# Recommender tower: two of the seven input blocks of dense layer 1 summed inside the interaction loop

## The reference

```python
e = jnp.stack([tbl_0[ids[:, 0]], ..., tbl_39[ids[:, 39]]], axis=1)
vi = e[:, i_idx, :]
vj = e[:, j_idx, :]
viW = jnp.einsum('bpd,pde->bpe', vi, W)          # W: 780 x 64 x 64
z = jnp.einsum('bpe,bpe->bp', viW, vj)           # 512 x 780
h = jnp.concatenate([z, dense_ctx], axis=1)      # 512 x 796
h = jnp.maximum(h @ W_top1 + b_top1, 0.0)        # 512 x 512
h = jnp.maximum(h @ W_top2 + b_top2, 0.0)        # 512 x 256
y = h @ W_top3                                   # 512 x 1
```

## Time and profile before

| | |
|---|---|
| median of 3 executions | 322.66 us (322.57, 322.66, 323.78) |
| span of the profiled execution | 320.2 us, 4340 instructions |
| its own time outside the span | not given apart; the median lies 2.5 us above the span |
| PE busy | 312.7 us (98%) |
| DVE busy | 252.3 us (79%) |
| POOL busy | 237.7 us (74%) |
| ACT busy | 90.3 us (28%) |
| granted TensorE clock | full in every slice (2.4 GHz) |

### The profile page before, as it was taken

How to read it: one execution, slowest core, us unless ns; L and a number is a source line. 1 busy time by engine, 2 the same in 40 slices (tenths; PEclk the granted TensorE clock), 3 DMA queues, 4 the chain that set the end, 5 groups by cost and what they waited for, 6 DMA issues and landing times.

```text
span 320.2 us, 4340 instructions
## 1 busy us (share of the span) xinstructions
PE 312.7 (98%) x1716; PEld 117.5 (37%) x1716; DVE 252.3 (79%) x243; ACT 90.3 (28%) x206; POOL 237.7 (74%) x178
## 2 busy tenths in 40 slices
PE   6899999999999999999999999999999999989996
PEld 2465233332333323333333333333333333323464
DVE  4995987788689888988898899999999999940000
ACT  0203500600106835559976363000000000000032
POOL 3898777777777777776677999999999999940000
PEclk9999999999999999999999999999999999999999
DMA  6981332323323753232323121221121000000000
GB/s 136 358 243 21 82 72 62 92 59 67 87 57 92 253 171 86 61 93 57 88 60 90 41 66 34 66 68 46 52 68 57 0 2 0 0 3 5 12 0 0
DMA packets 14459, 23.27 MB, mean 73 GB/s; under 512 B 3556, under 2 KB 4584, under 8 KB 14312
## 3 DMA queue, kind: packets, MB, share of 16 engines
q1 hardware_dynamic: 7848, 13.96, 15.6%
q0 software_dynamic: 4096, 4.20, 6.4%
q10 hardware_dynamic: 2496, 4.84, 4.5%
HBM read 22.86 MB, written 0.00 MB: 71 GB/s over the span
## 4 chain that ended last, share of the span: by engine, by line
PE 65%; POOL 28%; DMA 3%; DVE 1%; POOLq 1%; ACT 0%; issue 0%; ACTq 0%
PE y_ps L611 33%; POOL prod L352 28%; PE z_ps L632 16%; PE y_ps L642 5%; PE y_ps L535 3%; DMA prod<-in_tbl 2%; PE t_ps L642 2%; PE y_ps L682 2%; PE t_ps L535 2%; PE t_ps L587 1%; DMA prod<-hot_ids 1%; DVE prod L522 1%; POOLq L185 1%; PE t_ps L682 1%; DVE x_quad L463 0%; PE y_ps L691 0%
## 5 line engine op out<-in xcount | busy, mean ns | idle before, releaser
L611 PE MATMUL y_ps<-x,w 64*128 64x512 f32 x780 | 183.3, 605 | 0.2
L336 POOL DMA_INDIRECT gathered<-in_tbl,ids_sb x128 | 130.6, 1020 | 45.7 <-issue 28.5
L522 DVE TENSOR_TENSOR prod<-y_ps,x 128x1024 f32<-128x1024 f32 x89 | 103.2, 1218 | 20.5 <-PE y_ps L611 20.1
L522 DVE TENSOR_TENSOR prod<-y_ps,x_quad 128x1024 f32<-128x1024 f32 x96 | 110.7, 1217 | 4.4 <-PE y_ps L611 3.7
L611 PEld LDWEIGHTS y_ps<-x,w 64*128 64x128 f32 x780 | 70.0, 186 | 108.3 <-issue 79.1
L352 POOL TENSOR_TENSOR prod<-prod 128x1024 f32<-128x1024 f32 x46 | 106.9, 2374 | 0.3
L632 PE MATMUL z_ps<-prod,select 128*32 128x512 f32 x596 | 74.5, 600 | 1.3 <-POOL prod L352 1.3
L389 ACT COPY x<-x_fold 32x128 f32<-32x128 f32 x112 | 33.1, 296 | 18.1 <-DVE x_fold L491 16.9
L632 PEld LDWEIGHTS z_ps<-prod,select 128*32 128x32 f32 x596 | 14.4, 108 | 54.1 <-issue 37.6
L418 ACT COPY zT<-z_ps 128x512 f32<-128x512 f32 x6 | 3.5, 586 | 100.6 <-PE z_ps L632 100.6
L412 ACT COPY x_mix<-x 64x512 f32<-64x512 f32 x40 | 24.7, 617 | 0.7
(11 more groups left out here) (46 smaller groups left out, 87.5 us busy)
## 6 DMA issues: line engine op xcount, KB each, us to landing
w<-w_rows SPq DMA_DIRECT2D x48, 256.0 KB, 2.7
gathered<-in_tbl,ids_sb POOLq DMA_INDIRECT x128, 2.5
w<-w_rows ACTq DMA_DIRECT2D x1, 1792.0 KB, 8.0
prod<-in_tbl ACTq DMA_DIRECT2D x6, 256.0 KB, 8.5
prod<-hot_ids SPq DMA_DIRECT2D x4, 256.0 KB, 6.7
prod<-in_tbl ACTq DMA_DIRECT2D x4, 128.0 KB, 3.1
w<-w_rows ACTq DMA_DIRECT2D x1, 512.0 KB, 9.7
w<-w_rows SPq DMA_DIRECT2D x1, 192.0 KB, 2.3
```

What stands on the lines that cost most here:

```text
L336: nc.gpsimd.indirect_dma_start(gathered[:, slot, c, s * DIM:(s + 1) * DIM], None, tables[f][:, :], bass.IndirectOffsetOnAxis(ap=ids_sb[:, ...
L522: nc.vector.tensor_tensor(prod[:, d % PROD_SLOTS, :, :], y_ps[:, d % DUO_SLOTS, :, :], factor, ALU.mult).then_inc(prod_ready, 1)
L611: last = nc.tensor.matmul(y_ps[:, d % DUO_SLOTS, half, :], w[rows, r % W_SLOTS, d % ROUND, :], x[rows, units[half], :], start=True, stop=True)
```

## The change

Blocks 0 and 1 of layer 1 (all four column groups, 8 matmuls of 128x128 weights with 512 columns) move into rounds 18 to 25, one per round, ahead of the round's last duo, with `t_ps` as their bank. The order is m = 1, 2, 3, 0, two rounds each. After m = 1, 2 and 3 ACT copies the bank to the new tile `h1_part` (`save_part`, at the head of ACT's rounds 20, 22 and 24); the sums of m = 0 stay in `t_ps` and are continued at the end. So `t_ps` isn't free from round 18 on, and units 18 and 19, which PE transposed there in rounds 26 and 28, go the way of `FOLDED` (now 11 to 19).

Behind the loop `rest` is blocks 2 to 5. Their matmuls are put in between `sum_round(47)` and `sum_round(48)` in another order, block 6 of m = 1, 2, 3, 0 follows, and m = 3 and m = 0 end last. DVE adds `h1_part` to the banks of m = 1, 2 and 3 in place, and ACT's ReLU reads the result; that of m = 0 still reads `t_ps`. Layer 2 takes its inputs in the order 1, 2, 3, 0.

```diff
-FOLDED = range(11, 18)
+FOLDED = range(11, 20)
+EARLY_BLOCKS = 2
+EARLY = {18 + EARLY_BLOCKS * n + b: (m, b) for n, m in enumerate((1, 2, 3, 0)) for b in range(EARLY_BLOCKS)}
...
+            def save_part(m):
+                act.wait_ge(part_summed, m)
+                nc.scalar.copy(h1_part[:, m - 1, :], t_ps[:, :]).then_inc(part_saved, 1)
...
+                if r - 1 in EARLY:
+                    m, b = EARLY[r - 1]
+                    if m and b == EARLY_BLOCKS - 1:
+                        save_part(m)
...
-            for m in range(M1):
-                act.wait_ge(h1_summed, m + 1)
-                nc.scalar.activation(h1[m], h1_ps[m], ACT.Relu, bias=b1[:, m:m + 1]).then_inc(h1_ready, 1)
+            for m in range(1, M1):
+                act.wait_ge(h1_added, m)
+                nc.scalar.activation(h1[m], h1_part[:, m - 1, :], ACT.Relu, bias=b1[:, m:m + 1]).then_inc(h1_ready, 1)
+            act.wait_ge(h1_summed, M1)
+            nc.scalar.activation(h1[0], h1_ps[0], ACT.Relu, bias=b1[:, 0:1]).then_inc(h1_ready, 1)
...
+            dve.wait_ge(part_saved, M1 - 1)
+            for m in range(1, M1):
+                dve.wait_ge(h1_summed, m)
+                nc.vector.tensor_tensor(h1_part[:, m - 1, :], h1_part[:, m - 1, :], h1_ps[m], ALU.add).then_inc(h1_added, 1)
...
+            def layer1_early(m, b):
+                if m == 1 and b == 0:
+                    pe.wait_ge(w1_loaded, 32)
+                    pe.wait_ge(z_saved, EARLY_BLOCKS)
+                    pe.wait_ge(x_ready, FOLDED.start)
+                elif b == 0:
+                    pe.wait_ge(part_saved, m - 1 if m else M1 - 1)
+                done = nc.tensor.matmul(t_ps[:, :], w1[:, b, m * ROWS:(m + 1) * ROWS], zT[:, b, :],
+                                        start=b == 0, stop=m > 0 and b == EARLY_BLOCKS - 1)
+                if m and b == EARLY_BLOCKS - 1:
+                    done.then_inc(part_summed, 1)
...
+                    if r in EARLY and d == ROUND * r + ROUND - 1:
+                        layer1_early(*EARLY[r])
                     interact(d)
...
-            sum_round(len(plan.rounds) - LAG)
-            pe.wait_ge(w1_loaded, 32)
-            full = list(range(NBLK - 1))
-            layer1(0, full[:-1], first=True)
-            pe.wait_ge(z_saved, NBLK - 1)
-            layer1(0, full[-1:])
-            for r in range(len(plan.rounds) - LAG + 1, len(plan.rounds)):
-                sum_round(r)
-            for m in range(1, M1 - 1):
-                layer1(m, full, first=True)
-            for m in range(M1 - 1):
-                layer1(m, [NBLK - 1], last=True).then_inc(h1_summed, 1)
-            layer1(M1 - 1, [NBLK - 1], first=True)
-            layer1(M1 - 1, full, last=True).then_inc(h1_summed, 1)
+            rest = list(range(EARLY_BLOCKS, NBLK - 1))
+            pe.wait_ge(z_saved, NBLK - 2)
+            layer1(0, rest[:-1])
+            sum_round(len(plan.rounds) - LAG)
+            pe.wait_ge(prod_ready, ROUND * (len(plan.rounds) - 1) + 1)
+            layer1(1, rest[:1], first=True)
+            sum_round(len(plan.rounds) - 1)
+            layer1(1, rest[1:-1])
+            layer1(2, rest[:-1], first=True)
+            pe.wait_ge(z_saved, NBLK - 1)
+            layer1(1, rest[-1:])
+            layer1(2, rest[-1:])
+            pe.wait_ge(dense_loaded, 16 * M1)
+            pe.wait_ge(last_copied, 16 * 4 * M1)
+            layer1(1, [NBLK - 1], last=True).then_inc(h1_summed, 1)
+            layer1(2, [NBLK - 1], last=True).then_inc(h1_summed, 1)
+            layer1(3, [NBLK - 1], first=True)
+            layer1(0, [NBLK - 1])
+            layer1(3, rest, last=True).then_inc(h1_summed, 1)
+            layer1(0, rest[-1:], last=True).then_inc(h1_summed, 1)
```

More of the change, by code:

```diff
@@ L214, in dlrm_tower @@
         head = sb("head", [ROWS, M1 + M2 + M2 * QUAD])
+        h1_part = sb("h1_part", [ROWS, 3, BATCH])
         y_out = sb("y_out", [ROWS, BATCH // 4])
@@ L273, in dlrm_tower @@
         z_saved = sem("z_saved")
+        part_summed = sem("part_summed")
+        part_saved = sem("part_saved")
         last_copied = sem("last_copied")
         h1_summed = sem("h1_summed")
+        h1_added = sem("h1_added")
         h1_ready = sem("h1_ready")
@@ L659, in _ @@
                     sum_round(r - LAG)
+            rest = list(range(EARLY_BLOCKS, NBLK - 1))
+            pe.wait_ge(z_saved, NBLK - 2)
+            layer1(0, rest[:-1])
             sum_round(len(plan.rounds) - LAG)
-            pe.wait_ge(w1_loaded, 32)
-            full = list(range(NBLK - 1))
-            layer1(0, full[:-1], first=True)
-            pe.wait_ge(z_saved, NBLK - 1)
-            layer1(0, full[-1:])
-            for r in range(len(plan.rounds) - LAG + 1, len(plan.rounds)):
-                sum_round(r)
-            for m in range(1, M1 - 1):
-                layer1(m, full, first=True)
+            pe.wait_ge(prod_ready, ROUND * (len(plan.rounds) - 1) + 1)
[3 more added lines that the diff above has]
+            layer1(2, rest[:-1], first=True)
+            pe.wait_ge(z_saved, NBLK - 1)
+            layer1(1, rest[-1:])
+            layer1(2, rest[-1:])
             pe.wait_ge(dense_loaded, 16 * M1)
             pe.wait_ge(last_copied, 16 * 4 * M1)
-            for m in range(M1 - 1):
-                layer1(m, [NBLK - 1], last=True).then_inc(h1_summed, 1)
-            layer1(M1 - 1, [NBLK - 1], first=True)
-            layer1(M1 - 1, full, last=True).then_inc(h1_summed, 1)
+            layer1(1, [NBLK - 1], last=True).then_inc(h1_summed, 1)
[4 more added lines that the diff above has]
+            layer1(0, rest[-1:], last=True).then_inc(h1_summed, 1)
             def layer2(n, m):
-                for k in range(M1):
+                for turn, k in enumerate((1, 2, 3, 0)):
                     if n == 0 and m == 0:
-                        pe.wait_ge(h1_ready, k + 1)
+                        pe.wait_ge(h1_ready, turn + 1)
                     last = nc.tensor.matmul(h2_ps[n][m][:, batch_halves[n]], w2[:, k, m * ROWS:(m + 1) * ROWS],
-                                            h1[k][:, batch_halves[n]], start=(k == 0), stop=(k == M1 - 1))
+                                            h1[k][:, batch_halves[n]], start=(turn == 0), stop=(turn == M1 - 1))
                 last.then_inc(h2_summed, 1)
```

## The result

The changed kernel takes 326.98 us (median of four, 325.91 to 330.08) where the kernel before takes 322.62: a ratio of 1.0152, 95% interval 1.01 to 1.0203: slower by 1 to 2%. The prediction was 326.4. The profiled execution has a span of 325.4 us, predicted 323.9; the fastest one, with a mean granted clock of 1.0, has 324.0. The kernel before has slower executions at a lower mean clock too: of 23 in a later run the five at 0.989 took 325.75 to 327.98 us, the others 321.45 to 325.17.

A forecast was written before the change was run, and what follows sets the result against it. PE was taken to bound rounds 18 to 25, PE, DVE and POOL all full in rounds 28 to 47, PE alone behind the loop. Terms: 9.4 - 5.9 + 0.2 = +3.7 on 322.66, giving 326.4 us; 8-in-10 range 323.8 to 328.0.

The forecast's parts named there:

- One early matmul costs 1.27 us in the loop, 10.2 for eight: Rounds 18 to 25: each early matmul adds 0.86 us plus edges of 0.20 and 0.21; eight add 10.2 us.
- the two parts (0.20 and 0.21): Loop edges per early matmul: 0.20 us from tail blocks between sums, 0.21 us from product runs cut by transposes.
- The rival that the edges are free: Rounds 18 to 25: eight early matmuls cost only 6.9 us, total 323.1; edges free or cheap, chance 0.13.
- PE has no slack in rounds 18 to 25: PE alone sets these 5.49 us rounds; DVE idles 0.87 us each, so nothing hides the early matmuls.
- The rival had named the right condition: PE has 0.87 us free per round in rounds 18 to 25: early matmuls cost 3.2 us, total 319.4; chance 0.06.
- Transposes and fold: Rounds 26 and 28: PE loses two times 0.59 us, DVE gains two times 0.70; PE's loop end 9.4 us later.
- The tail, 20.5 us: From the end of round 46's sums to layer 2: 20.5 us against 26.34, 5.9 shorter, including a 2.1 us new wait.
- The rival without a new wait: Tail: block 6's copies land sooner, so PE doesn't wait; +1.6 us, total 324.3; chance 0.05.
- The partial sums, 0.2 us: Layer 2: DVE's add and ReLUs delay PE by 0.2 us (0.1 to 0.8); ACT's m = 2 save has 2.3 slack.
- "The granted clock is full, so nothing below hangs on it.": Whole kernel: granted clock full (2.4 GHz) in every slice and window before the change, so no term depends on it.

The follow-up runs named there:

- the half-row kernel: Changed kernel with early matmuls using only the upper 64 rows of weights and block (result unusable): 354.04 us, one execution, chip with late DVE starts.
- the two matmuls in a row: Changed kernel with the eight early matmuls placed two at a time at the head of rounds 18, 20, 22, 24: 356.39 us against 357.73 before.
- ten matmuls ahead: Changed kernel with three more m = 3 matmuls before block 6, ten instead of seven: 323.94 us against 322.88; on a late-DVE chip 350.91 against 357.35.
- the filled wait: Changed kernel plus two useless matmuls in PE's wait for block 6: 351.91 us against 357.35 for the kernel before, ratio 0.9851.
- tail and folds: Kernel before with five m = 0 matmuls ahead of round 47's sums and units 18, 19 turned on DVE, no early matmuls: 320.55 us against 322.88.
- the tail alone: Kernel before with only five finished m = 0 matmuls moved ahead of round 47's sums: 355.95 us against 357.35, ratio 0.9956, late-DVE chip.
- the folds alone: Kernel before with only units 18 and 19 turned on DVE instead of PE: 356.89 us against 357.35, ratio 0.9955.
- the changed kernel again: Changed kernel rerun without edit on another chip: 326.51 us against 322.75 for the kernel before, ratio 1.0114.

## Why the prediction was right, point by point

- **One early matmul costs 1.27 us in the loop, 10.2 for eight.** Measured 1.26 and 10.05. I had called the two parts (0.20 and 0.21) two pairs of edges; the half-row kernel and the two matmuls in a row show that each is one change of shape, into layer 1 and back into the products. The rival that the edges are free would have had rounds of 6.34, and it falls.
- **PE has no slack in rounds 18 to 25.** Right where the prediction was made: 6.74 us a round and not 5.9. On the chips with late DVE starts PE has slack, and there the change with ten matmuls ahead or with the filled wait is 1.5 to 1.7% faster. The rival had named the right condition.
- **Transposes and fold.** PE's loop end came 9.15 us later (290.87 against 281.72), predicted 9.4: 10.05 - 0.59 - 0.59 + 0.37, and the loop reached round 18 0.09 earlier. The 0.25 that I had too much are 0.15 in the early matmuls, 0.09 in that start, and rounding; PE ran into its slots for 0.37 us where I had taken 0.4.
- **The tail, 20.5 us.** 20.86 at the full clock. The resume of PE, 8.3 us after the sums of round 48, came at 8.4 (298.53 to 306.94) and at 8.7 in the other execution; the new wait was 2.13 and 2.44 us, predicted 2.1. The rival without a new wait falls.
- **The partial sums, 0.2 us.** From layer 2's start to ACT's last copy it is 0.22 us more (314.06 to 323.14 against 309.05 to 317.91). ACT's save of m = 2 lay at 157.17, some 3 us before PE needed the bank.
- **"The granted clock is full, so nothing below hangs on it."** This step was wrong. It was true of the kernel before and I took it over to the changed one, whose tail has a wait that the old one lacked. In one of its two traced executions the clock is halved for 3.4 us behind that wait and the kernel pays 1.4 us more. That is why the profiled span is 325.4 while the fastest one, 324.0, lies at my 323.9. What I could have done: where a step adds idle time to PE, price the matmuls behind it at both clocks.

The sum at the full clock: +9.15 - 5.48 + 0.22 = +3.9, predicted +3.7. That it is so near is in part luck: the loop came 0.25 us below my term and the tail 0.4 us above.

The balance of the change, then: 1.9 us gained by tail and folds, 3.2 lost by the edges of the early matmuls, 2.1 to 2.4 lost by the wait, 0.2 by the partial sums, and 1.4 more when the clock falls in the tail.

## What to carry to other kernels

Work that is moved from a stretch where the engine works alone into one where it is the bound gains nothing by itself; ask what it costs at the new place, above all in edges: a matmul of another array shape between two runs costs its streaming time and here 0.2 us for each of two changes. Several in a row, at a place where the shape changes anyway, pay for fewer (0.96 us each instead of 1.26), but check that they then don't hold up the engine behind: on the chip with late starts these rounds got longer by it. Count what the moved work was hiding where it stood, here the copies of the last block. And measure such a change on more than one chip: the kernel with ten matmuls ahead was 0.4% slower than the kernel before on one and 1.7% faster on another, where DVE is late.

## What the runs showed of the hardware that I had not expected

- A wait of 2.13 us of a PE that had been busy throughout was followed, 0.8 us after its end, by a granted clock of 0.50 for 3.4 us. Outside rounds 0 to 3 the kept traces have seven single waits of 2.1 to 2.6 us. Within 1.2 us of the end of five of them the clock fell to 0.50 (2.13 in the changed kernel, 2.57 in the tail alone, 2.59 in the folds alone, 2.44 in the tail of two at the head and of half rows); after two of 2.44 it stayed at 1.00 (the changed kernel again, and round 18 of two at the head). After more than 30 waits of 1.0 to 1.85 us it stayed at 1.00 too, and between round 4 and the end of PE's work it never fell without a wait of 2.1 us or more. So the wait and the fall go together, but what decides after a wait of 2.44 us stays open.
- On some chips DVE starts products late by 1 to 3 us while its operands are there and no semaphore explains it; in the tail-alone kernel most of the late starts from round 8 on come within 0.4 us after the last transfer of a gather. The kernel before takes 35 us more on these chips. The cause stays open: no run separated the DMA from the chip.
- PE's change of array shape cost 0.20 us into layer 1 and 0.20 us into the products. Into the sums it cost less: 8 records take 0.99 us and 16 take 1.85, which leaves 0.13 for the change.
